# A layer of delta-rule attention and FFN on one core: work groups as halves, and narrower waits for the FFN keys and the channel mixing

## The reference

```
outs = [dwconv_causal(x, w) for w in (ms_w3, ms_w15, ms_w31)]
y = concatenate(outs) -> per head 3*128 columns
y = y @ kernel_mix_w                      # per head
y = y.reshape(b, l, h * d) @ channel_mixer_w   # over all four heads
```

```
xr = mu_r * x + (1 - mu_r) * x_prev;  xk = mu_k * x + (1 - mu_k) * x_prev
r = sigmoid(xr @ W_r.T);  k = square(relu(xk @ W_k.T));  out = r * (k @ W_v.T)
```

## Time and profile before

| | |
|---|---|
| time, median of 3 runs | 3507.43 us (3506.42 to 3511.52) |
| span of the profiled execution | 3507.7 us |
| TensorE (PE) busy | 3329.3 us, 95% |
| TensorE weight loads (PEld) | 2457.7 us, 70% |
| VectorE (DVE) busy | 3165.0 us, 90% |
| ScalarE (ACT) busy | 2760.5 us, 79% |
| GpSimd (POOL) busy | 826.6 us, 24% |
| instructions | 70018 |

### The profile page before, as it was taken

How to read it: one execution, slowest core, us unless ns; L and a number is a source line. 1 busy time by engine, 2 the same in 40 slices (tenths; PEclk the granted TensorE clock), 3 DMA queues, 4 the chain that set the end, 5 groups by cost and what they waited for, 6 DMA issues and landing times.

```text
span 3507.7 us, 70018 instructions
## 1 busy us (share of the span) xinstructions
PE 3329.3 (95%) x22880; PEld 2457.7 (70%) x22880; DVE 3165.0 (90%) x7841; ACT 2760.5 (79%) x9146; POOL 826.6 (24%) x1501
## 2 busy tenths in 40 slices
PE   7999999999999999999999999999999999999988
PEld 6666777677776677776677766777766777766764
DVE  6998999999988999899999989999899999999994
ACT  5777888777887778887788877788877788777775
POOL 3322221122221222211222212222112222122211
PEclk9999999999999999999999999999999999999999
DMA  6012211122211222111222112222112221112211
GB/s 187 19 39 51 51 40 34 29 51 51 50 32 29 42 51 51 38 35 29 51 51 49 32 26 46 51 51 41 33 29 51 51 50 33 33 38 51 45 30 21
DMA packets 188307, 154.92 MB, mean 44 GB/s; under 512 B 111804, under 2 KB 146108, under 8 KB 187688
## 3 DMA queue, kind: packets, MB, share of 16 engines
q0 software_dynamic: 31744, 79.70, 13.2%
q1 hardware_dynamic: 156200, 70.76, 7.7%
HBM read 51.34 MB, written 52.95 MB: 30 GB/s over the span
## 4 chain that ended last, share of the span: by engine, by line
PE 35%; ACT 22%; DVE 21%; issue 9%; DMA 8%; POOL 4%; SPq 0%; ACTq 0%; DVEq 0%; POOLq 0%
DVE my L1804 16%; PE dense L798 7%; PE dense L732 5%; PE dense L736 5%; DMA my<-prod 5%; PE dense L720 3%; ACT my L1272 3%; PE small L748 2%; ACT dense L1302 2%; PE cell L702 2%; DMA rows_out<-Bm 2%; PE cell L703 2%; PE cell L695 2%; POOL Xu L464 1%; DMA Bu<-rows_out 1%
## 5 line engine op out<-in xcount | busy, mean ns | idle before, releaser
L1804 DVE SCALAR_TENSOR_TENSOR my<-vT,mw,my 128x256 f32<-128x256 f32 x5408 | 2256.4, 482 | 38.3 <-DMA my<-prod 19.9
L422 POOL TENSOR_SCALAR vare<-xsq 128x2 f32<-128x2 f32 x32 | 6.0, 188 | 2026.7 <-ACT xsh L1022 2026.7
L798 PE MATMUL dense<-xsh,w 128*128 128x256 f32 x2016 | 474.5, 381 | 3.8
L798 PEld LDWEIGHTS dense<-xsh,w 128*128 128x128 f32 x2016 | 362.6, 190 | 70.9 <-ACT xr L1334 10.9
L1245 ACT ACTIVATE ka<-dense 128x512 f32<-128x512 f32 x64 | 38.2, 597 | 309.0 <-PE dense L720 309.0
L720 PE MATMUL dense<-xk,wfk 128*128 128x256 f32 x1024 | 245.3, 394 | 16.7 <-DVE xb L1864 14.3
L720 PEld LDWEIGHTS dense<-xk,wfk 128*128 128x128 f32 x1024 | 195.9, 196 | 67.2 <-issue 40.5
L574 PE MATMUL front<-xsh,wq 128*128 128x256 f32 x1024 | 237.6, 385 | 0.6 <-ACT raw L1060 0.6
L732 PE MATMUL dense<-wr,xr 128*128 128x512 f32 x512 | 235.3, 603 | 0.0
L574 PE MATMUL front<-xsh,wv 128*128 128x256 f32 x1024 | 229.9, 382 | 2.7 <-ACT xsh L1037 2.7
L736 PE MATMUL dense<-wfv,ka 128*128 128x512 f32 x512 | 230.2, 592 | 0.0
(11 more groups left out here) (188 smaller groups left out, 6855.9 us busy)
## 6 DMA issues: line engine op xcount, KB each, us to landing
my<-prod POOLq DMA_DIRECT2D x160, 384.0 KB, 4.2
xa<-in_x SPq DMA_DIRECT2D x32, 512.0 KB, 4.4
rows_out<-Bm SPq DMA_DIRECT2D x64, 256.0 KB, 4.2
out<-xb POOLq DMA_DIRECT2D x32, 512.0 KB, 14.8
Yq<-units_out SPq DMA_DIRECT2D x128, 32.0 KB, 2.3
w<-in_w SPq DMA_DIRECT2D x1, 2048.0 KB, 16.7
Bu<-rows_out SPq DMA_DIRECT2D x32, 64.0 KB, 3.0
units_out<-Xu SPq DMA_DIRECT2D x32, 64.0 KB, 2.5
```

The costliest lines, as they stand in the source:

```text
L798: e.matmul(by_batch(o), w1[:, k, hs(2 * pair + c)], xsh[s % 2][:, k, :, 1:1 + P], start=(k == 0), stop=False)
L1804: i = e.scalar_tensor_tensor(o, vT[s % 2][:, c, :, off:off + P], mw[:, col:col + 1], o, ALU.mult, ALU.add)
```

## The change

Every function that issued a group is split, so that a call issues a half of the group or a single item, and the lists call the parts one behind the other in the old place. For most groups this leaves instructions, order and waits as they are. What differs:

- `mix_half(s, j)` and `mix_in(s, j, c)`: `xk` (j = 1) comes before `xr` (j = 0) on both engines; `mixed_half` counts two per slice; each `mix_in` item waits for its half and for the shifted column.
- `ffn_key` waits for the first four of `mixed_in`. `gate_out`, the first half of the old `ffn_out`, waits for all eight. `value_out(s, 1)` waits for `gated(s, 0)` too.
- `channel_mix`: the first two heads' matmuls wait for `mix_done` of heads 0 and 1, the other two for all.
- `copy_o` and `copy_ms`: the wait for `f_rest(s-1)` moves from before the copy to before the sums.

```diff
-        mixed_half, mixed_in = signal("mixed_half"), signal("mixed_in", 2 * CB)
+        mixed_half, mixed_in = signal("mixed_half", 2), signal("mixed_in", 2 * CB)
...
+            def ffn_key(s, pair, c):
+                if c == 0:
+                    if s == 0:
+                        e.wait_ge(ffn_in, 48)
+                    e.wait_ge(*mixed_in.upto(s, CB - 1))
+                    if s:
+                        e.wait_ge(*xb_done.upto(s - 1, pair))
                 for k in range(CB):
+                    i = e.matmul(dense[pair][:, c * W:(c + 1) * W], wfk[:, k, hs(2 * pair + c)], xk[:, k, :],
+                                 start=(k == 0), stop=(k == CB - 1))
+                if c == 1:
+                    i.then_inc(key_mm.sem, 1)
+
+            def gate_out(s, b, part):
+                if part == 0:
+                    e.wait_ge(*mixed_in.upto(s))
+                    if b == 0:
+                        e.wait_ge(*key_relu.upto(s, 0))
+                    else:
+                        e.wait_ge(*gated.upto(s, 0))
+                for k in range(2 * part, 2 * part + 2):
                     i = e.matmul(dense[0][:, :], xr[:, k, hs(b)], wr[:, k, :], start=(k == 0), stop=(k == CB - 1))
...
+            def value_out(s, b, part):
+                if part == 0:
+                    e.wait_ge(*key_done.upto(s))
+                    if b == 1:
+                        e.wait_ge(*gated.upto(s, 0))
...
+            def channel_mix(s, b, part):
+                if part == 0:
+                    if s == 0:
+                        e.wait_ge(cm_in, 16)
+                    e.wait_ge(*mix_done.upto(s, 1))
+                    e.wait_ge(*(gate_tanh, gated)[b].upto(s))
+                else:
+                    e.wait_ge(*mix_done.upto(s))
+                for k in range(2 * part, 2 * part + 2):
                     i = e.matmul(dense[b][:, :], ym[:, k, hs(b)], cm[:, k, :], start=(k == 0), stop=(k == CB - 1))
...
-            def mix_half(s):
+            def mix_half(s, j):
...
                 if s:
-                    e.wait_ge(*key_mm.upto(s - 1))
-                    e.wait_ge(*gate_mm.upto(s - 1))
+                    e.wait_ge(*(gate_mm, key_mm)[j].upto(s - 1))
                     e.wait_ge(*logits_mm.upto(s - 1))
-                for j, dst in enumerate((xr, xk)):
-                    for c in range(CB):
-                        i = e.activation(by_batch(dst[:, c, :]), xsh[s % 2][:, c, :, 1:1 + P], ACT.Copy, scale=mu[:, j, c:c + 1])
+                dst = (xr, xk)[j]
+                for c in range(CB):
+                    i = e.activation(by_batch(dst[:, c, :]), xsh[s % 2][:, c, :, 1:1 + P], ACT.Copy, scale=mu[:, j, c:c + 1])
                 i.then_inc(mixed_half.sem, 1)
...
-                mix_half(i - 1)
+                mix_half(i - 1, 1)
+                mix_half(i - 1, 0)
...
+            def mix_in(s, j, c):
+                e.wait_ge(*mixed_half.upto(s, 1 - j))
                 if s == 0:
                     e.wait_ge(mix_rest, 1)
                 else:
                     e.wait_ge(*shifted.upto(s - 1))
...
-                mix_in(i - 1)
+                mix_in(i - 1, 1, 0)
+                mix_in(i - 1, 1, 1)
+                mix_in(i - 1, 1, 2)
+                mix_in(i - 1, 1, 3)
+                mix_in(i - 1, 0, 0)
...
-                taps(i - 2, 3, 11, 13)
+                taps(i - 2, 3, 11, 12)
+                taps(i - 2, 3, 12, 13)
```

More of the change, by code:

```diff
@@ L710, in state @@
                 i.then_inc(kTu_mm.sem, 1)
[L712 to L722, removed]
@@ L782, in begin_last_hidden, with hidden @@
                                      xsh[s % 2][:, k, :, 1:1 + P], start=(c == 0 and k == 0), stop=False)
[L784 to L787, removed]
+            def hidden(s, pair, c):
                 last = s == NS - 1
                 begun = last and pair < 2
[L790 to L802, removed]
+                if c == 0:
+                    if s == 0:
+                        e.wait_ge(fusion_in, 64)
+                        e.wait_ge(scaled, N_SCALED)
+                    if pair < 2 or last:
+                        e.wait_ge(*ms_done.upto(s, pair % 2))
+                    else:
+                        e.wait_ge(*hid_done.upto(s, pair - 2))
+                o = hidden_bank(s, pair)[:, c * W:(c + 1) * W]
+                if not begun:
+                    for k in range(CB):
+                        e.matmul(by_batch(o), w1[:, k, hs(2 * pair + c)], xsh[s % 2][:, k, :, 1:1 + P], start=(k == 0),
+                                 stop=False)
+                e.wait_ge(*f_done.upto(s))
+                i = e.matmul(o, w1x[:, hs(2 * pair + c)], ftT[:, :], start=False, stop=(c == 1 or not begun))
+                if c == 1:
+                    i.then_inc(hid_mm.sem, 1)
             def logits(s, half):
@@ L867, in tensor_program @@
             join_W(0)
-            project(1, 4)
+            project(1, 4, 0)
+            project(1, 4, 1)
             join_Z(0)
-            ffn_out(0, 0)
+            gate_out(0, 0, 0)
+            gate_out(0, 0, 1)
+            value_out(0, 0, 0)
+            value_out(0, 0, 1)
             half_W(0)
@@ L879, in tensor_program @@
                 outputs(i - 2, 1)
-                ffn_out(i - 2, 1)
+                gate_out(i - 2, 1, 0)
+                gate_out(i - 2, 1, 1)
+                value_out(i - 2, 1, 0)
+                value_out(i - 2, 1, 1)
                 state(i - 2, 0)
@@ L924, in tensor_program @@
                 join_Z(i - 1)
-                ffn_out(i - 1, 0)
+                gate_out(i - 1, 0, 0)
+                gate_out(i - 1, 0, 1)
+                value_out(i - 1, 0, 0)
+                value_out(i - 1, 0, 1)
                 half_W(i - 1)
@@ L933, in tensor_program @@
             outputs(NS - 2, 1)
-            ffn_out(NS - 2, 1)
+            gate_out(NS - 2, 1, 0)
+            gate_out(NS - 2, 1, 1)
+            value_out(NS - 2, 1, 0)
+            value_out(NS - 2, 1, 1)
             state(NS - 2, 0)
@@ L961, in tensor_program @@
             query_key(NS - 1, 1)
-            attend(NS - 2, 0)
+            attend(NS - 2, 0, 0)
+            attend(NS - 2, 0, 1)
             turn_o(NS - 2, 1)
             key_state(NS - 1, 1)
-            attend(NS - 2, 1)
-            ffn_key(NS - 1, 0)
-            ffn_key(NS - 1, 1)
-            ffn_out(NS - 1, 0)
+            attend(NS - 2, 1, 0)
+            attend(NS - 2, 1, 1)
+            ffn_key(NS - 1, 0, 0)
+            ffn_key(NS - 1, 0, 1)
+            ffn_key(NS - 1, 1, 0)
+            ffn_key(NS - 1, 1, 1)
+            gate_out(NS - 1, 0, 0)
+            gate_out(NS - 1, 0, 1)
+            value_out(NS - 1, 0, 0)
+            value_out(NS - 1, 0, 1)
             inverse_W(NS - 1)
@@ L973, in tensor_program @@
             join_Z(NS - 1)
-            ffn_out(NS - 1, 1)
+            gate_out(NS - 1, 1, 0)
+            gate_out(NS - 1, 1, 1)
+            value_out(NS - 1, 1, 0)
+            value_out(NS - 1, 1, 1)
             half_W(NS - 1)
@@ L1424, in scalar_program @@
             copy_beta(0)
+            copy_bq(0)
             tanh_beta(0)
@@ L1925, in vector_program @@
             taps(0, 2, 35, 36)
-            mix_in(0)
+            mix_in(0, 1, 0)
+            mix_in(0, 1, 1)
+            mix_in(0, 1, 2)
+            mix_in(0, 1, 3)
+            mix_in(0, 0, 0)
+            mix_in(0, 0, 1)
+            mix_in(0, 0, 2)
+            mix_in(0, 0, 3)
             taps(0, 2, 16, 17)
```

560 lines of the change are left out of this document (376 added, 184 removed).

## The result

The changed kernel took 3523.09 us, the median of 7 runs (3511.20 to 3532.12), against 3507.43 us for the kernel before (3501.90 to 3515.26): 1.004 times, with an interval of 1.0021 to 1.006. The forecast was 3510, with 3499 to 3520 around it. It was too low, and the result lies outside the range.

What follows compares the result with a forecast made beforehand. The prediction took TensorE's order together with the waits in it as the bound (busy 95% of the span). Its terms, -0.3 - 0 + 0 + 2 + 1 = +2.7 us, gave 3510.1, stated as 3510, range 3499 to 3520.

Steps and rivals of the forecast that it cites:

- the lead: VectorE starting mix_in earlier in 7 stages, 5.8 us together; claimed to be given back at the my<-prod DMA, 0.
- Part 1: Token mix, xk before xr: keys wait for four activations, not eight; the gain is given back before Wq, 0.
- the third rival: Idle time moves into the inverse burst, clock may fall: likely +3, at most +8; 0.60 with forecast and fourth rival.
- stage 2's stop: TensorE stop for issue at L639, then clock 0.50 for 6.8 us, costing up to 3.4 us.
- places: Distances of TensorE's 256-instruction block boundaries from the inverse burst's first instruction; 244, 250, 0, 6, 12 predicted in five stages.
- Part 2: Last stage's channel_mix starts with two heads of ym, removing a 0.46 us wait: -0.3 us.
- Part 3: Wait instructions added by splitting on VectorE, TensorE and ScalarE stay hidden: 0; 7 us if all on the path.
- Part 4: Moved TensorE instruction-block boundaries in the inverse burst: +2 us for longer stops, +1 for the low clock behind them.
- The second rival: Full stops in the inverse burst of stages 16, 23, 30, 7.0 us each, not 3.8: 3517 to 3523, chance 0.26.
- The dangerous stretch: Part of the inverse burst where a block boundary can stop TensorE; five stages lie in it, as before, 3.8 us each.

Runs made afterwards that it cites:

- lead_undone: The changed kernel with VectorE's mix_in waiting for both of ScalarE's halves again, as before; 0.9981 of the kernel before.
- waits_only: The kernel before with only the change's three added TensorE wait instructions per stage; 0.998 of the kernel before, 1.0018 when repeated.
- those named under "`Wq` earlier": Profiles of the changed kernel (1.004, 1.0008, 1.0021), of it with keys waiting for all of mixed_in (1.0029), and with channel_mix waiting for all four heads (1.002).
- even_bad: The kernel before with 77 more TensorE wait instructions per stage and 54 at the start, block boundary at 248 in every stage; 1.0184 of the kernel before.
- the two again: Repeats, beside the changed kernel on one chip, of lead_undone (1.0007 of the kernel before) and waits_only (1.0018).
- channel_whole: The changed kernel with channel_mix's first part waiting for all four heads of mix_done again; 1.002 of the kernel before.
- even_160: The kernel before with 77 more TensorE wait instructions per stage and 142 at the start, block boundary at 160 in every stage; 0.9947 of the kernel before.
- the two kernels with the swap: turn_Y and mask_W moved two taps earlier on VectorE: in the changed kernel, 1.0006; in the kernel before with the boundary at 160 in every stage, 0.997.
- lead_undone_again: Repeat of lead_undone beside the changed kernel on one chip; 1.0007 of the kernel before.
- after_again: The changed kernel unaltered, measured once more on a second chip; 1.0008 of the kernel before.

## Why the prediction was wrong

**The mean over all runs.** The kernel before has 127 runs in all, mean 3513.8 (standard error 0.7), the changed kernel 31, mean 3518.8 (1.6): the change costs 5.0 us (1.7). Without the first comparison it is 3.5 (2.0). `lead_undone` and `waits_only`, which have its TensorE instructions without the lead, have 47 runs, mean 3513.2 (1.5; one execution of 9378 us is left out). So the changed kernel is 5.5 us (2.2) above them, and they are not above the kernel before. These errors take the runs as independent, and that flatters them: the same two kernels were 6.7 us (2.3) under the kernel before when measured first and 4.1 us (2.4) over it the second time, on the same chip. Measured together, the difference by the lead was 0.0014 and 0.0003, inside the intervals. The lead's cost is therefore likely, but not shown by a single comparison.

**Luck.** Of the 15.7 us between the first medians some 12 are spread: the 7 runs of before were 6 us under the median of its later 120 (3513.6), those of after 6 over that of its own later 24 (3516.9). By those later runs the changed kernel lies inside the range, and 3.3 us above the kernel before where I had 2.7. That the number missed is mostly the draw; the mechanism was mis-sized all the same.

**Part 1, keys first: right in what happens, wrong in its sum of 0.** The waits went, the lead met the DMA, the idle time moved into the burst, as written. The step that failed is the third rival: "the clock may fall there, at half of stage 2's 3.4 us each, 1.7", in "likely one or two" stages, which the sum left at 0. In five profiles (those named under "`Wq` earlier") nine stages with the lead stood 1.0 us or more for `Wq` and ran low-clock, one to three in each. They took 108.9 to 110.5 us, one 113.9, the middle one 109.2, so 3.7 over 105.46: 1.7 in the second key pair, 1.2 where the clock reads low once more, in `key_state` and the multiplication behind it (L689, L696), and 0.6 to 1.0 of longer idle time in the burst. In the profile shown there are three: 3 x 3.7 = 11 in place of 3. A part comes back, as waits before the keys go (5.8 to 2.0 us in `mix_in`, 14.3 to 10.9 for `xb`). And not all of the 11 is the lead's: stage 18 took 109.3 us before as well, and stage 11, the one of 113.9, stands 4.3 us for `dl` of ScalarE (L1472) near its end, for a reason that I did not look for. The trace of the kernel before had the row that priced it, stage 8, where a late `my<-prod` made TensorE wait 1.5 us for `Wq` and the stage took 109.3; I read stage 2's stop instead:

```profile
954.53 0.72 PE L639 MATMUL cell<-Wq,Xq 32*32 32x16 f32 x64 [1.51 <-DVE Wq L1749]
955.18 5.41 PE L720 MATMUL dense<-xk,wfk 128*128 128x256 f32 x16
```

Over 16 profiles (all but `even_bad`), 33 of the 41 stages in which TensorE stood 1.0 us or more for `Wq` were low-clock, against 61 of 423 others, and 53 of these 61 had a stop for "issue". Without the lead, five profiles with moving places (`before`, `lead_undone`, `waits_only` and the two again) have 6 low-clock stages with such a stand, the five with the lead 14. That is 1.6 more in each, some 6 us; the 29 stages together are 3113.3 us on average with the lead and 3110.3 without, so about half of it comes back.

**Part 2: right.** The wait for `ym` in the last stage went and came back in `channel_whole`; 0.3 us is below what a run tells.

**Part 3: right.** Undisturbed stages are unchanged: the three shortest take 105.37 to 105.44 us, where they took 105.41 to 105.43. They have 12 wait instructions more (7 on VectorE, 3 on TensorE, and 2 on ScalarE, where I had 1); `mix_in`'s four take 1.70 and 1.66 us as they took 1.67. `even_160` carries 77 more on TensorE in each stage, and its undisturbed stages take 105.49.

**Part 4: the places right, the price not.** In the profile shown, stages 2, 9, 16 and 23 took 438.13 us together, 16.5 over 4 x 105.42, where five had taken 19.05 more before; I had forecast 3 more. The 19.05 was mis-read in part: stage 12's 3.9 of it lie outside the burst (its second key pair took 3.72 us, at full clock; TensorE stood 2.1 us for `dl` of ScalarE late in the stage). `waits_only` in two comparisons gives 0.998 and 1.0018, so nothing that can be measured. The second rival, full stops at places 0, 6 and 12, held for one of the three: in the nine profiles with these places stage 16 always stopped, 0.7 to 3.5 us, and in five of them took 113.0 to 113.5 us; stage 23 stopped at most 1.8, stage 30 once, 0.4. The dangerous stretch was drawn too narrow: stages 5, 12, 19 and 26, at places 210 to 228, stopped in some of these profiles (stage 19 in six of the nine, for 0.8 to 2.1 us), though not in the first one. Even place 248 in every stage costs 2.6 a stage, not 7.0. The Trainium skill ("Runtime: NRT & Kernel Launch", Instruction fetch mechanics) has block crossings mostly hidden. The runs say that it depends: at place 160 they are, in every stage; at 248 they cost 2.4% (1.0184/0.9947).

**The range.** "A run can tell from no change about 0.2%" was drawn from three runs within 5 us. The later 120 runs of before lie between 3494 and 3535 us, and their time follows the mean granted clock, 3.2 us for each 0.001 of it. One low-clock stage, 3.7 us, is about that. An execution has 3 to 9 such stages in these profiles (`even_bad` and the two kernels with the swap left out), and a change of the sort studied here moves their odds. Their number alone does not give the time: `lead_undone_again` has 6 and its 29 stages took 3125.9 us, `after_again` 9 and 3115.7. The range of 21 us was narrower than the spread of the runs alone.

## What to carry to other kernels

Where a transfer lands at a fixed time, an engine that gets ahead upstream of it only moves idle time: ask into which stretch it goes, and price it by a stage of the same trace that already has the idle time in that stretch. Where the body of an unrolled loop is near a multiple of 256 TensorE instructions, or can be padded to one, choose where the boundary falls: away from bursts of tiny matmuls, and so that the fetch doesn't come due under a big store. Before a forecast within half a per cent, look at how much executions of one kernel differ, not at three runs.

## What the runs showed of the hardware beyond expectation

- Wait instructions on TensorE that are long met cost nothing to be seen ahead of wide matmuls: 77 more in a stage of 105.49 us, against 105.46 without them.
- 88 instructions more in the prologue, nothing else, took 75.7 us off the 29 stages (`even_bad` to `even_160`), which began 4.3 us later.
- At places 212 and 214 the packet, 16 KB, of the block that begins in the burst started at most 4 us after the boundary before it when it got ahead of the 512 KB store, 5.2 to 8.1 us after it when the store had begun. Elsewhere in a stage a packet started as late as 6.1 us after a boundary without a stop, where the next boundary was not near.
- All 105 stops for "issue" of 0.3 us or more ended 2.2 to 4.0 us after the start of a packet of TensorE's instruction queue.
- TensorE's granted clock fell after it had stood 1.2 us or more for `Wq` in 24 of 27 stages (16 profiles); the second key pair's window then reads 0.68 in most of them.
